# Expert weights applied ahead of the down product, with all 18 down products added up in one PSUM bank

## The reference

```python
# x: layer-normed rows; 16 experts (E), width 128 (F), 4 groups, top 2 groups, top 4 experts
topk_idx, tw = _route(x, router_w, bias)            # sigmoid scores, tw = scores / sum * 2.5
combine = (one_hot(topk_idx, E) * tw[..., None]).sum(1)           # [tokens, 16]
h = einsum('td,edf->etf', x, gate_w);  u = einsum('td,edf->etf', x, up_w)
y = einsum('etf,efd->etd', silu(h) * u, down_w)
routed = einsum('etd,te->td', y, combine)
sh = silu(x @ sh_gate_w) * (x @ sh_up_w) @ sh_down_w              # two shared experts
out = x_in + routed + sh
```

## Time and profile before

| | |
|---|---|
| median of 3 runs | 2417.89 us (2417.57 to 2418.84) |
| profiled execution, its own time | 2417.1 us from the first to the last instruction (the profile gives no other time for it) |
| PE busy | 2207.2 us, 91% |
| DVE busy | 1870.2 us, 77% |
| ACT busy | 1085.0 us, 45% |
| POOL busy | 595.7 us, 25% |
| experts_phase | from about 1684 us to the end |

### The profile page before, as it was taken

The page is one execution under the profiler, slowest core; times in us unless marked ns, Lnnn a source line. Parts: engine busy times, 40 slices in busy tenths (PEclk is TensorE's granted clock), DMA queues, the critical chain, the costliest instruction groups (busy, mean ns, idle before and its releaser), DMA issues. The chain is left out here.

```text
span 2417.1 us, 50766 instructions
## 1 busy us (share of the span) xinstructions
PE 2207.2 (91%) x17730; PEld 1618.7 (67%) x17730; DVE 1870.2 (77%) x4892; ACT 1085.0 (45%) x2116; POOL 595.7 (25%) x552
## 2 busy tenths in 40 slices
PE   6999996787769999997999999897699999999998
PEld 3666664566645555554566666575588888888887
DVE  5888886767747888887688888565788888888886
ACT  3555552555534444442454545343344444344443
POOL 1111110000002323332223333265422322223222
PEclk9999997999979999998899999899799999999999
DMA  3000000000000000000100000100000000000000
GB/s 113 27 26 26 17 9 1 1 1 0 0 1 1 1 0 0 0 0 18 27 27 17 26 17 9 59 0 0 1 10 5 5 9 5 5 9 5 9 5 9
DMA packets 47055, 30.28 MB, mean 13 GB/s; under 512 B 10480, under 2 KB 45552, under 8 KB 46704
## 3 DMA queue, kind: packets, MB, share of 16 engines
q1 hardware_dynamic: 46960, 29.18, 4.0%
HBM read 24.98 MB, written 4.19 MB: 12 GB/s over the span
## 5 line engine op out<-in xcount | busy, mean ns | idle before, releaser
L609 PE MATMUL ps<-kblk,qd 128*128 128x512 f32 x768 | 407.8, 613 | 0.0
L354 ACT ACTIVATE ex<-ps 128x512 f32<-128x512 f32 x384 | 229.3, 597 | 395.0 <-PE ps L624 393.6
L1145 ACT ACTIVATE moe_sg<-ps 128x512 f32<-128x512 f32 x288 | 172.6, 599 | 365.4 <-PE ps L1197 365.3
L459 DVE TENSOR_REDUCE mx<-ps 128x8 f32<-128x512 f32 x384 | 262.6, 684 | 73.0 <-PE ps L616 26.6
L1181 PEld LDWEIGHTS ps<-down,moe_act 128*128 128x128 f32 x2048 | 266.0, 191 | 32.9 <-DVE moe_acc L1374 12.5
L624 PEld LDWEIGHTS ps<-pack,sh 128*128 128x128 f32 x1536 | 179.6, 140 | 152.1 <-issue 95.6
L1181 PE MATMUL ps<-down,moe_act 128*128 128x128 f32 x2048 | 271.2, 275 | 5.8 <-DVE moe_acc L1374 5.8
L461 DVE TENSOR_TENSOR sh<-ps,mx 128x512 f32<-128x512 f32 x384 | 265.6, 692 | 13.1
L641 PEld LDWEIGHTS ps<-vblk,ex 128*64 128x64 f32 x6144 | 210.2, 137 | 64.6 <-issue 63.8
L641 PE MATMUL ps<-vblk,ex 128*64 128x32 f32 x6144 | 252.9, 225 | 0.3
L1356 DVE TENSOR_TENSOR moe_act<-ps,moe_sg 128x512 f32<-128x512 f32 x288 | 197.8, 687 | 68.7 <-PE ps L1197 54.9
(11 more groups left out here) (241 smaller groups left out, 4118.1 us busy)
## 6 DMA issues: line engine op xcount, KB each, us to landing
cin<-in_ctx SPq DMA_DIRECT2D x32, 256.0 KB, 3.2
x_res<-in_x SPq DMA_DIRECT2D x16, 256.0 KB, 3.0
out<-moe_acc SPq DMA_DIRECT2D x16, 256.0 KB, 2.3
pack<-in_pack SPq DMA_DIRECT2D x1, 2474.5 KB, 8.9
kmi<-in_key_mask SPq DMA_DIRECT2D x16, 128.0 KB, 3.0
kmi<-in_key_mask SPq DMA_DIRECT2D x32, 64.0 KB, 2.9
wqkv<-in_wqkv SPq DMA_DIRECT2D x1, 1536.0 KB, 8.5
gate<-in_gate SPq DMA_DIRECT2D x6, 192.0 KB, 4.0
```

Of the source, the lines that this page charges most:

```text
L354: nc.scalar.activation(ex[:, u % 2], TB[u % 2].rearrange("p (c n) -> p c n", n=P), ACT.Exp).then_inc(e_ready, 1)
L459: nc.vector.tensor_reduce(mx[:, u % 2], sc, AX.X, ALU.max).then_inc(max_done, 1)
L609: last = nc.tensor.matmul(SB[w], qd[:, s, w, t * P:(t + 1) * P], kblk[:, s, 2 * t + w].rearrange("p h k -> p (h k)"), start=True, stop=a == 0)
L1145: nc.scalar.activation(sg[:, k % 2], GB_[k % 2], ACT.Silu).then_inc(silu_done, 1)
```

## The change

In experts_phase the routing weight no longer multiplies the result of the down product but the rows that go into it. The down product is turned around: down[k] is the 128 x 128 weights, and the 512 columns of act_ stream through, so the result has the feature on partitions and the token on columns, and all 18 experts of a group add up in one PSUM bank, YB[s]. The weight of a token is then needed on every partition, as a row. So comb is transposed on PE (`turn_weights`, slot 15), copied by ACT (combT), stored to a small array in DRAM by four DMAs and loaded back by 16 DMAs, each of which repeats one expert's row of 512 on all 128 partitions (`spread_weights` on SP; the buffer wide_w is the memory of y_res, which is free by now). POOL multiplies silu's result with that row (`weigh`, 16 a group) into wsg, and DVE multiplies wsg in place of sg with the up bank. DVE's `accumulate`, ACT's `weigh_expert` and POOL's `add_part` and `total` are gone. At the end ACT copies the sum (yT), PE transposes its four tiles back (`turn_sum`, slot 6 of the next group), and DVE adds x (`add_up`, slot 7). PE's gate product now waits only for silu of two experts earlier, the up product for act_ of two experts earlier. The routing parts move to slots 6, 7, 8, 8, 9, 10, 13, 14; rank_experts is in slot 11 of POOL.

```diff
         @block.sync
+            def spread_weights(g, more):
+                sp.wait_ge(combT_copied, nth(g))
+                if more:
+                    for e in range(E):
+                        sp.wait_ge(wide_loaded[e], g * 16)
+                for t in range(TILES):
+                    sp.dma_start(comb_dram[:, t * P:(t + 1) * P], combT[t * E:(t + 1) * E, :]).then_inc(comb_kept, 16)
+                sp.wait_ge(comb_kept, nth(g) * 16 * TILES)
+                for e in range(E):
+                    if more:
+                        sp.wait_ge(weighed, (g - 1) * E + (e + 1))
+                    sp.dma_start(wide_w[:, e, :], comb_dram[e:e + 1, :].partition_broadcast(P)
+                                 ).then_inc(wide_loaded[e], 16)
...
         @block.gpsimd
-            def add_part(g, j):
-            def total(g, s):
+            def weigh(g, e):
+                k = e + SH
+                pool.wait_ge(silu_done, nth(g, K, k))
+                pool.wait_ge(wide_loaded[e], nth(g) * 16)
+                if e >= 2:
+                    pool.wait_ge(act_ready, nth(g, K, k - 2))
+                nc.gpsimd.tensor_tensor(wsg[:, e % 2], sg[:, k % 2], wide_w[:, e, :], ALU.mult).then_inc(weighed, 1)
...
             def step(g, s, first, more):
+                for k in range(K):
+                    if k >= SH:
+                        weigh(g, k - SH)
+                    if more and k == 1:
+                        scale_rows(g + 1)
+                    if more and k == 4:
+                        low_rows(g + 1, 1 - s)
+                    if more and k == 11:
+                        rank_experts(g + 1)
...
         @block.scalar
                     act.wait_ge(g_ready, nth(g, K, k))
+                    if k >= SH + 2:
+                        act.wait_ge(weighed, nth(g, E, k - 2 - SH))
+                    elif k >= 2:
+                        act.wait_ge(act_ready, nth(g, K, k - 2))
...
         @block.tensor
+            def turn_weights(g):
+                pe.wait_ge(routing, nth(g, NR, NR - 1))
+                nc.tensor.transpose(CB, comb[:, :, :].rearrange("p a e -> p (a e)"), C["ident"]).then_inc(combT_ready, 1)
...
-                    for t in range(TILES):
-                        last = nc.tensor.matmul(YB[k % 2][:, t * D:(t + 1) * D], act_[:, k % 3, t * P:(t + 1) * P],
-                                                down[:, k, :], start=True, stop=True)
+                last = nc.tensor.matmul(YB[s], down[:, k, :], act_[:, k % 3], start=k == 0, stop=k == K - 1)
...
                     if k >= 2:
+                        pe.wait_ge(silu_done, nth(g, K, k - 2))
+                    elif not first:
+                        pe.wait_ge(silu_done, g * K + (k - 1))
+                    product(GB_[k % 2], gate_hi[:, k], gate_lo[:, k], x_hi[:, s], x_lo[:, s]).then_inc(g_ready, 1)
+                    if k >= 2:
                         pe.wait_ge(act_ready, nth(g, K, k - 2))
...
-                    product(GB_[k % 2], gate_hi[:, k], gate_lo[:, k], x_hi[:, s], x_lo[:, s]).then_inc(g_ready, 1)
                     product(UB[k % 2], up_hi[:, k], up_lo[:, k], x_hi[:, s], x_lo[:, s]).then_inc(u_ready, 1)
...
+                    if not first and k == TURN_Y:
+                        turn_sum(g - 1)
+                    if more and k == 15:
+                        turn_weights(g + 1)
...
         @block.vector
-                dve.wait_ge(silu_done, nth(g, K, k))
+                if k < SH:
+                    dve.wait_ge(silu_done, nth(g, K, k))
+                else:
+                    dve.wait_ge(weighed, nth(g, E, k - SH))
-                V.tensor_tensor(act_[:, k % 3], UB[k % 2], sg[:, k % 2], ALU.mult).then_inc(act_ready, 1)
+                V.tensor_tensor(act_[:, k % 3], UB[k % 2], sg[:, k % 2] if k < SH else wsg[:, k % 2], ALU.mult
+                                ).then_inc(act_ready, 1)
-            def accumulate(g, s, k):
+            def add_up(g, s):
-            ROUTE_SLOTS = (6, 7, 8, 9, 10, 11, 14, 16)
+            ROUTE_SLOTS = (6, 7, 8, 8, 9, 10, 13, 14)
```

More of the change, by code:

```diff
@@ L915, with experts_phase @@
 CH = 3
-def experts_phase(nc, ps, C, x_res, gate, up, down, w_loaded, out):
+def experts_phase(nc, ps, C, x_res, y_res, gate, up, down, w_loaded, comb_dram, out):
     with ExitStack() as ctx:
@@ L995, in experts_phase @@
         routing = sem("routing")
[L996 removed]
+        comb_set = sem("comb_set")
+        combT_ready = sem("combT_ready")
+        combT_copied = sem("combT_copied")
+        comb_kept = sem("comb_kept")
+        wide_loaded = [sem(f"wide_loaded{e}_") for e in range(E)]
         g_ready = sem("g_ready")
@@ L1119, in high_weights, with copy_combT, copy_yT @@
                     nc.scalar.copy(up_hi[:, part], up[:, part]).then_inc(w_high, 1)
+            def copy_combT(g, first):
+                act.wait_ge(combT_ready, nth(g))
+                if not first:
+                    act.wait_ge(comb_kept, g * 16 * TILES)
+                nc.scalar.copy(combT[:, :], CB).then_inc(combT_copied, 1)
+            def copy_yT(g, s):
+                act.wait_ge(yT_ready, nth(g))
+                nc.scalar.copy(yT[:, :], YB[s]).then_inc(yT_copied, 1)
             def prep(g, s):
@@ L1124, in prep @@
                 route_exp(g, s)
[L1126 to L1136, removed]
-                for t in range(TILES):
-                    last = nc.scalar.activation(part[:, j, t], YB[k % 2][:, t * D:(t + 1) * D], ACT.Copy,
-                                                scale=comb[:, s, t, k - SH:k - SH + 1])
-                last.then_inc(acc_done, 1)
+                copy_combT(g, True)
             def step(g, s, first, more):
@@ L1151, in step @@
                         route_exp(g + 1, 1 - s)
+                    if more and k == 15:
+                        copy_combT(g + 1, False)
+                if not more:
+                    copy_yT(g, s)
             pipelined(act, NG, prep, step)
@@ L1172, in prep, with down_proj, turn_sum @@
                 logits(g, s)
-            def down_proj(g, k, first):
+                turn_weights(g)
+            def down_proj(g, s, k, first):
                 pe.wait_ge(act_ready, nth(g, K, k))
[L1176 to L1180, removed]
-                        last = nc.tensor.matmul(YB[k % 2][:, t * D:(t + 1) * D], act_[:, k % 3, t * P:(t + 1) * P],
-                                                down[:, k, :], start=True, stop=True)
[L1183 to L1192, removed]
+                if k == 0 and not first:
+                    pe.wait_ge(yT_copied, g - 1)
+                    pe.sem_inc(passed, 1)
+                last = nc.tensor.matmul(YB[s], down[:, k, :], act_[:, k % 3], start=k == 0, stop=k == K - 1)
+                if k == K - 1:
+                    last.then_inc(yT_ready, 1)
+            def turn_sum(g):
+                pe.wait_ge(yT_copied, nth(g))
+                for t in range(TILES):
+                    last = nc.tensor.transpose(XB[:, t * P:(t + 1) * P], yT[:, t * P:(t + 1) * P], C["ident"])
+                last.then_inc(y_ready, 1)
             def product(out, hi, lo, x, y):
@@ L1389, in step @@
                         norm_stats(g + 1, 1 - s)
-                    if more and k == 2:
+                    if more and k == 1:
                         norm_apply(g + 1, 1 - s)
+                    if not first and k == ADD_Y:
+                        add_up(g - 1, 1 - s)
                     for part, at in enumerate(ROUTE_SLOTS):
@@ L1395, in step @@
                 if not more:
-                    for k in range(K - 3, K):
-                        accumulate(g, s, k)
+                    add_up(g, s)
+            V.memset(comb[:, :, :], 0.0).then_inc(comb_set, 1)
+            dve.wait_ge(comb_set, 1)
             pipelined(dve, NG, prep, step)
@@ L2052, in build @@
                     for i in range(K // CH) for buffer, array in ((gate, gate_in), (up, up_in), (down, down_in))])
-        experts_phase(nc, ps, C, x_res, gate, up, down, w_loaded, out)
+        experts_phase(nc, ps, C, x_res, y_res, gate, up, down, w_loaded, comb_dram, out)
 def kernel(**inputs):
```

127 lines of the change are left out of this document (53 added, 74 removed).

## The result

The changed kernel takes 2507.14 us (median of 4 runs, 2506.75 to 2508.3), beside 2417.85 us of the kernel before on the same chip: 1.0369 times as long, 95% interval 1.0354 to 1.0383. The prediction was 2512, slower, in a range of 2434 to 2560. The profiled execution took 2506.75 us with a span of 2505.0, 6 under the 2511 predicted for the span.

A forecast was written before the change was run, and what follows sets the result against it. PE was taken as the bound. Start 1715.4 + 2.6, fifteen group starts 744 (48.4 + 14 x 49.1 + 8) and end 49 gave a 2511 us span, so 2512 us, 94 slower; range 2434 to 2560.

The forecast's parts named there:

- PE's own work: Experts' stage: 18 down products at 0.87 plus added transposes, +0.2 us a group; laid out 42.3 us without stalls.
- The four waits: PE stalls per group, in order: up(11) 1.4, up(12) 1.1, up(14) 3.1, turn_weights in slot 15 1.2; sum 6.8 us.
- The port: SBUF's port: a short DVE instruction with both inputs in SBUF stands until POOL's ends, 1.22 us in place of 0.22.
- the walk: One group stepped through at 2.25 us a step, DVE and POOL each waiting for the port: 42.3 + 6.8 = 49.1.
- DVE's jump of the loop: DVE's 2.2 us at the loop's jump delay norm_apply and make_xT by 1.3 us in 6 groups, +8.
- 48.4 + 2.6: Start of the stage: first group 48.4 us, and half clock from gate(0) costs about 2.6 us more.
- Rival (c): Experts' stage: the stalls bring PE's clock down, 33 us more, 2545; chance 0.12.
- the end: Last group: 42.3 us to its last act_, then down, copy, transposes, add and store; 49 us.
- The DMAs: Loading repeated rows, 16 DMAs of 256 KB a group on SP: hidden, with 3 us to spare.
- (a): Port costs little because short routing instructions fall into POOL's pauses: 44.7 us a group, 2437; chance 0.15.
- (b): Not slower: with (a), POOL also works faster, weigh 1.10 us; period 43.4, 2417; chance 0.08.

The follow-up runs named there:

- the best version: Changed kernel with rank_experts on DVE, make_xT, logits and exp one slot earlier, routing spread singly over slots 5 to 14, transpose in slot 16: 2396.47 us.
- three of the experiments: Best kernel with rank_experts back on POOL: 2471.29 us; changed kernel with POOL's multiplies read by nobody: 2484.34; that with rank_experts on DVE: 2478.34.

## Why the prediction was right

**PE's own work.** Right: 42.3 laid out, 42.31 without weighing, 42.22 in the best version; a down pair takes 2.24 - 6 x 0.23 = 0.86 (0.87 predicted). Merging 18 products in one bank and the added transposes nearly cancel, as said.

**The four waits.** Between gate products at full clock: 3.64 - 2.24 = 1.40 (predicted 1.4), 3.43 - 2.24 = 1.19 (1.1), 5.34 - 2.24 = 3.10 (3.1), and at the transpose 3.96 - 2.69 = 1.27 (1.2), where 2.69 is the same step without weighing on POOL. Together 7.0 us, and 49.27 - 42.31 is 7.0. Each went when its named cause was taken away: the third by moving rank_experts, the first, second and fourth by leaving the routing out, and all four by taking POOL's multiplies away. Moving the transpose took the fourth wait away too, but not its time.

**The port.** Right in both directions: DVE ends 0.08 to 0.09 after POOL (L1352, L1364, TENSOR_SCALAR L1321 at 0.80 on average, 0.18 alone), and POOL waits for DVE too (2.10 for 1.28), which the walk had assumed without a row. The prediction counts 18 routing instructions as exposed to the port, the four tensor_scalar among them; by its own definition there are 22 in the program. In the changed kernel four or five a group are caught (L1321, L1340, L1352, L1364, and L1383 in some groups). The Trainium skill, "SBUF — State Buffer", section "Who interferes with whom", says that a VectorE instruction with two SBUF inputs and a GpSimd instruction that reads SBUF shut each other out for a whole instruction, and that issue order decides who waits; the traces agree, with 1.27 for 0.225 us one way and 2.10 for 1.28 the other.

**Where it was off.** Three terms of the sum were wrong and small. The 8 us for DVE's jump of the loop did not come: before, DVE stood up to 2.2 us there; after, all idle time of its act_ that nothing explains is 0.2 us, and PE's step with make_xT takes 3.0 us in every group. The first group took 49.65 us in place of 48.4 + 2.6; the half clock did cost its first two steps 2.5 us, but they have no down product to make (1.7 us), and the 48.4 takes off only 0.7 in all. And the clock was taken at 1.00: it falls to half once in every second group, after the 2.8 us wait.

```profile
2050.00:2051.00 1.00, 0.60 (x2) 0.56 (x3) 0.46 (x2) 0.25 (x1) 1.00 (x2) 0.86 0.00 0
2051.00:2052.00 1.00, 1.00 (x3) 0.73 (x3) 1.00 (x2) 0.00 (x0) 1.00 (x1) 0.50 0.00 0
...
2053.00:2054.00 1.00, 1.00 (x3) 0.61 (x2) 0.96 (x4) 0.00 (x0) 0.00 (x0) 0.50 0.00 0
2054.00:2055.00 1.00, 1.00 (x5) 0.77 (x5) 0.40 (x2) 0.34 (x1) 0.00 (x0) 0.93 0.00 0
```

A fall costs 1.2 to 1.7 us (47.35 - 45.74 = 1.6, 48.1 to 48.5 less 46.9, 47.88 - 46.23 in three of the experiments), but in the changed kernel only 49.61 - 49.27 = 0.34 net, because it spares the 1.3 at the transpose. Rival (c) was thus half right: its mechanism came, at some 3 us in place of 33. The Trainium skill, "TensorE: Matmul & The Clock Gate", section on HAM oscillation, was cited for it: its rule that each burst pays again holds in the changed kernel in every second group alone, and with the transpose moved in every group.

In sum, from first gate product to first gate product: 15 starts of groups took 2455.67 - 1713.87 = 741.8 us, predicted 744 + 2.6; the first began at 1713.9, not 1715.4; the end took 49.3, predicted 49. That is 1.5 + 4.8 - 0.3 = 6 under the predicted span. The 4.8 is in part luck: the jump's 8 and 1.3 of the first group were too much, and 14 groups of 49.44 in place of 49.1 (half of it waits, half the clock) put 4.8 back.

**The DMAs.** Hidden, as said, with nearly the margin computed. The first row, for which 3.0 was assumed, lands 3.1 to 3.5 us after its issue, and 2.4 to 2.9 us before its weighing (1.7 in the last group), where 3 was computed. The rows behind it take longer, 6.3 at the median of all, but are needed later; an issue takes 0.37 at the median in place of 0.61.

**What the prediction did not see.** It took (a) and (b) as matters of how large the port's waits are. They are rather a matter of where the routing stands: the port's waits stay in the best version and cost nothing. What delays act_ in the changed kernel is that eight routing instructions stand in slot 8, two of them caught (L1340 and L1352), and the comparison which starts rank_experts comes behind that queue. With the same instructions spread, but no earlier, the waits at steps 11 and 12 were gone; only that kernel also has rank_experts on DVE, which by itself left them in place.

## What to carry to other kernels

Before an engine is put into a chain that runs once per step, lay its existing long blocks beside the slack of a step: 4.4 us against 1.5 cost 2.0 to 3.5 us a group, however much air there was elsewhere, and in the spread schedule the same work cost nothing on DVE. Where two engines catch each other as here, a short instruction of the one can cost a whole instruction of the other; spread such instructions over the steps, and early, so that their waits fall in pauses. And a change that frees an engine which was not the bound gives nothing back until the freed time is used, here to take the block from POOL.

## What the runs showed of the hardware

- After some of PE's waits its clock was at half for the next three microseconds. The kernels whose longest wait was 1.1, 1.6, 1.7 and 1.8 us kept 1.00; those with a wait of 2.1, 2.7, 2.8 and 3.2 us a group had the fall in 13 of 15 groups, in about two of three, in every second (or, with the transpose moved, in every one) and in about three of four. What picks the groups was not settled.
- Two such kernels can trade a wait for a fall of the clock and take the same time (2507.1 and 2507.2); a comparison of the times alone would have read this as no effect.
- A 64-element instruction of DVE with two inputs in SBUF costs what POOL's instruction has left: L1352 took 1.257 to 1.284 us in place of 0.225 in all 15 groups of the stage, so the cost repeats with the schedule and does not scatter.
